# GpSimd makes four of z's sixteen low parts instead of VectorE

## The chip, the core and the metric

The kernel runs on one core of a Trainium2 chip (trn2). Its time is the device time of one execution in microseconds. The engines are called PE (TensorE), DVE (VectorE), ACT (ScalarE), GpSimd or POOL, and SP (the queue that issues most DMAs). They run on their own and meet only at semaphores.

## The reference

The input x is (32, 64, 1024). Two blocks are added to it in turn:

```python
x = x + attn(cond(x, cond_128, ...), w_attn, w_proj, adapter_wte, gating)
x = x + ffn(cond2(x, cond_128, ...), W_base, b_base, W_router, A, B)
```

`cond` mixes the 64 channels of each batch entry with a 64x64 matrix of its own (a softmax over 8 expert matrices, from a small MLP on cond_128) and adds a bias: `out = einsum('boi,bih->boh', agg_w, x) + agg_b`. Its result is called z here: 2048 tokens (32 batches of 64) by 1024. `attn` projects z to q, k and v (1024 to 3 x 1024), rotates q and k, does causal attention over the 64 tokens of each batch entry with 32 heads of 32, adds attention to ten adapter rows, and projects back. `cond2` is a grouped convolution along the 1024, and `ffn` a 1024x1024 layer with a top-2 choice of rank-16 adapters. Everything is float32.

## The kernel before, in words

PE multiplies in the reduced format fp32r. To keep float32's precision, a big operand is split in a high part (a copy rounded to fp32r) and a low part (the float32 value minus the high part), and each product is three matmuls: high by high, high by low, low by high (`split_passes`, line 80). So each piece of z needs a high and a low part in SBUF before it can be projected.

**z in sixteen pairs.** z is made two batch entries at a time: pair i, for i from 0 to 15, is 128 partitions by 1024. Four pairs make a unit u of 512 tokens: unit 0 is pairs 0 to 3, unit 1 is 4 to 7, unit 2 is 8 to 11, unit 3 is 12 to 15. A pair takes four steps on three engines:

- mix i, on PE (lines 269 to 281): 32 small products (64 matmul records) of x with the mixing matrix, into PSUM. It waits for x by DMA and for add i-2 (`wait(pe, z_sum, i - 1)`), since pairs alternate over two sets of PSUM banks. It counts z_mm up.
- add i, on DVE (lines 357 to 369): PSUM plus bias, to f_z_raw in SBUF. One instruction of 1024 for even i (line 363), two of 512 for odd i (line 367). It counts z_sum up.
- high i, on ACT (lines 317 to 319): copy of f_z_raw to fp32r in z. It waits for add i and counts z_hi up.
- low i, on DVE (lines 371 to 373): f_z_raw minus the high part, to z, all three tiles in SBUF. It waits for high i and counts z_lo up.

**The order on PE** is written out by hand. `first_step` (lines 1085 to 1099) does mixes 0 to 5, waits for the lows of unit 0 (`split(0)`), and then projects unit 0 of the first weight group to K, Q and V in eight chunks each; behind every second chunk stands another mix: 6 to 9 in K, 10 to 13 in Q, 14 and 15 in V. Between Q and V lies the small product `project_adapter`. Afterwards `unit_step` (lines 981 to 1001) runs 31 times, for 8 weight groups g by 4 units u: for g = 0 it waits first for the lows of its unit (`mix_tensor.split`, line 283), then come the attention scores of the unit before (lines 893 to 908, which wait for the rotated q and k and for a_avs), the transposes of v (line 964, which wait for ACT's copy vT), the projections K and Q, the transposes of the softmax's results (lines 913 and 920), the projection V, and the products of attention and values (line 935). Each projection is 24 matmuls of 128x512 (line 952). After the attention follow 16 groups of matmuls for the output projection and the ffn (line 1030).

**The order on DVE** is that of its instructions in the code: `mix_on(0, UP)` and the next lines (1345 to 1354) do adds 0 to 4 and lows 0 to 3; `unit_step` with n = 0 does adds 5 to 10 with lows 4 to 9 (line 1619), the rotation of K (`rotate`, lines 1364 to 1382: a product of PSUM and cosine, line 1372; a shuffle out of PSUM, 1374; a product of two SBUF tiles, 1377; a sum of two SBUF tiles, 1380 or 1382), adds 11 to 14 each followed by the low before it (line 1628), the rotation of Q, add 15 (line 1633), the three small instructions a_avs, a_avh, a_avbd (lines 1646 to 1651), and low 14 (line 1655). With n = 1 come the softmax of unit 0 (`attend_softmax`, lines 1384 to 1430: for two halves a masked sum out of PSUM, 1396, a maximum, 1399, a subtraction of two SBUF operands, 1401, and so on to 1430), both rotations and low 15 (line 1635).

**The order on ACT**: highs 0 to 3, a copy of Q's weights, highs 4 to 6, a copy of V's, highs 7 to 10 (lines 1160 to 1167), then in `unit_step` with n = 0 highs 11 to 13, a small copy, high 14, another, high 15 (line 1274), and vT (line 1282), which PE's transposes wait for.

**The order on GpSimd** (lines 856 to 886): a small clear, the low parts w_lo of the three weight blocks (line 379, each after ACT's high part), a clear of aprob once eight adds are done, a clear of vbd once all sixteen mixes are done (line 865; ACT's first copies into vbd wait for it), and then nothing until the ffn, where it adds a bias to 16 tiles (line 879).

**SP** loads x pair by pair into four buffers (a load waits for the mix that frees its buffer), and after the last mix three constants (lines 671 to 673).

Of the kernel before, what the change touches and what calls it, by code (L numbers as in the profile page):

```python
# [27 lines left out]
ALU = mybir.AluOpType  # L28
# [13 lines left out]
UP = UB // 2  # L42
KC = L // P
NP = NB // 2
# [23 lines left out]
Q_, K_, V_ = 0, 1, 2  # L68
MLP_COLS = (NB, P, 1, P, 1, NM, NC)
MIX_COLS = (OB * NC, P // NM)  # L70
DMA_RING = 1024


def wait(eng, sem, value):

    if not isinstance(value, int) or value > 0:
        eng.wait_ge(sem, value)
# [20 lines left out]
def split_columns(t, widths):  # L98

    ends = np.cumsum(widths)  # L100
    return [t[:, int(e - w):int(e)] for w, e in zip(widths, ends)]


def mixing(nc, ctx, d, psum, z, z_f, z_raw, ctx_dram, aggb_dram, first_weights, places):
# [8 lines left out]
    def sem(name):  # L113
        return ctx.enter_context(nc.semaphore(name))
# [15 lines left out]
    sb = Space(nc, "m", small_at).take  # L130
    mix = sb("mix", [P, sum(MIX_COLS)])
    mixw, pick = split_columns(mix, MIX_COLS)
    h0 = sb("h0", [P, NB])
# [35 lines left out]
    z_sum = sem("m_z_sum")  # L169
    z_hi = sem("m_z_hi")  # L170
    z_lo = sem("m_z_lo")
    NCONST = 5
    HALVES = ((0, UP), (UP, NP))

    def slot_bank(i, b):

        return bank[(0, 1, 2, 4)[2 * (i % 2) + b]]

    def z_place(z, i, part):

        return z[:, i // UP, part, :, i % UP * P:(i % UP + 1) * P]
# [42 lines left out]
    class Tensor:  # L224
# [6 lines left out]
        def begin(pe):  # L231
# [9 lines left out]
            pe.wait_ge(mlp_act, 2)  # L241
            pe.wait_ge(consts, 16 * NCONST)
            pe.wait_ge(ones_set, 1)
# [37 lines left out]
            mm.then_inc(z_mm, 1)  # L281

        def split(pe, u):
            pe.wait_ge(z_lo, UP * (u + 1))

    class Scalar:

# [33 lines left out]
    class Vector:  # L321

        def begin(dve):
            dve.memset(busy[:].bitcast(F32), 1.0).then_inc(busy_set, 1)
            dve.memset(ones[:], 1.0).then_inc(ones_set, 1)
            dve.wait_ge(consts, 16 * NCONST)
            dve.wait_ge(ctx_mm, 1)
# [47 lines left out]
    class Pool:  # L375

        def weight_lo(pool, x):
            pool.wait_ge(w_hi[x], 1)
            pool.tensor_tensor(wlo[:, :, x, :], wst[:, :, x, :], whi_f[:, :, x, :], ALU.subtract).then_inc(w_lo[x], 1)

    return (Sync, Pool, Tensor, Scalar, Vector), ctx_out, z_mm, z_sum


def program(nc, d, psum, z, zbase, y_dram, x1_dram, w_forms, ctx_dram, aggb_dram, weights, out):
# [8 lines left out]
    with ExitStack() as ctx:  # L393
        def sem(name):
            return ctx.enter_context(nc.semaphore(name))
# [146 lines left out]
        y_out = sem("a_y_out")  # L542
        NCONST, NCLEAR, NFCONST = 10, 3, 3

# [57 lines left out]
        mix_sync, mix_pool, mix_tensor, mix_scalar, mix_vector = parts  # L602
# [3 lines left out]
        def first(g, u):  # L606
            return isinstance(g, int) and g == 0 and u == 0
# [4 lines left out]
        def refill(g, u):  # L612

            return u == NU - 1 and not last(g)
# [5 lines left out]
        def prep_at(n):  # L620

            g, u = n // NU, n % NU
            return 2 * g + u - 1 if u in (1, 2) else None
# [9 lines left out]
        def plain(f):  # L633

            t, half = {A11: (0, 0), A12: (0, 1), A21: (1, 0), A22: (1, 1)}[f]
            return raw[:, t, KH * half:KH * (half + 1), :]
# [16 lines left out]
        def form_count(order, f, G):  # L653

            return sum(len(order(i)) for i in range(G)) + order(G).index(f) + 1
# [200 lines left out]
        @block.gpsimd  # L856
        def _(pool):
            pool.memset(wte[:, KC * NA:], 0.0).then_inc(cleared, 1)
            mix_pool.weight_lo(pool, K_)
            mix_pool.weight_lo(pool, Q_)  # L860
            mix_pool.weight_lo(pool, V_)
            pool.wait_ge(z_sum, 2 * UP)
            pool.memset(aprob[:].bitcast(F32), 0.0).then_inc(cleared, 1)
            pool.wait_ge(z_mm, NP)
            pool.memset(vbd[:], 0.0).then_inc(cleared, 1)


            def add_bias(G, t):
                if G == NJ and t == 0:
                    pool.wait_ge(row1_set, 2)  # L870
                elif G == NJ:
                    pool.wait_ge(row2_set, 1)
                elif t == 0:
                    pool.wait_ge(x_in[0], 16 * G)
                    pool.wait_ge(row1_set, 2 * G - 1)
                else:
                    pool.wait_ge(x_in[1], 16 * G)
                    pool.wait_ge(v2_set, G)
                pool.tensor_tensor(xn[:, t, :].rearrange("p (m q) -> p q m", q=PH),  # L879
                                   x1[:, t, :].rearrange("p (q m) -> p q m", q=PH),  # L880
                                   bbase[:].rearrange("p (m q) -> p q m", q=PH), ALU.add).then_inc(xn_set, 1)

            pool.wait_ge(fconsts, 16 * NFCONST)
            for G in range(NJ, 2 * NJ):
                for t in range(2):
                    add_bias(G, t)

        @block.tensor
        def _(pe):
# [77 lines left out]
            def project_adapter(g, n):  # L967
                if g == 0:
                    pe.wait_ge(consts, 16 * NCONST)
                    pe.wait_ge(cleared, 1)  # L970
# [372 lines left out]
        def _(dve):  # L1343
            mix_vector.begin(dve)
            def mix_on(i0, i1):

                for i in range(i0, i1):
                    mix_vector.add(dve, i)
                    if i:
                        mix_vector.low(dve, i - 1)  # L1350

            mix_on(0, UP)
# [3 lines left out]
            def split_lo(x, g, n):  # L1356
                dve.wait_ge(w_hi[x], g + 1)
                wait(dve, mm_done[x], n)
                if x != Q_:
                    wait(dve, akv_mm, g)  # L1360
                dve.tensor_tensor(wlo[:, :, x, :], wst[:, :, x, :], whi_f[:, :, x, :], ALU.subtract
                                  ).then_inc(w_lo[x], 1)
# [69 lines left out]
            def prep_sums(k):  # L1432

                dve.wait_ge(prep_in, 32 * (k + 1))
                part = prep_raw

                def take(dst, a, b, done):
                    wait(dve, prep_sum, done)
                    dve.tensor_tensor(part[:, dst, :], part[:, a, :], part[:, b, :], ALU.subtract).then_inc(prep_sum, 1)

                take(T3, B22, T1, 0)
                take(T1, T1, B11, 0)
                take(T2, B22, T1, 4 * k + 2)
                take(T4, B21, T2, 4 * k + 3)
# [29 lines left out]
            def low(G, f):  # L1474
                dve.wait_ge(act_hi_set, form_count(form_order, f, G))
                src = act_sum[f][:] if f in (S1, S2, S4, S3) else plain(f)
                dve.tensor_tensor(act_lo[f][:], src, act_hi[f][:].bitcast(F32), ALU.subtract).then_inc(act_set, 1)  # L1477
# [138 lines left out]
            def unit_step(g, u):  # L1616
                n = NU * g + u
                if n == 0:
                    mix_on(UP + 1, NP - 5)
                if n == 1:  # L1620
                    dve.wait_ge(cleared, 2)
                if not first(g, u):
                    attend_softmax(n - 1)
                if n == 0:
                    dve.wait_ge(consts, 16 * NCONST)
                rotate(K_, bK, kr, n, ((scores, 2 * n),), n)
                if n == 0:
                    mix_on(NP - 5, NP - 1)
                if prep_at(n) is not None:
                    prep_sums(prep_at(n))  # L1630
                rotate(Q_, bQ, qr, n, ((scores, 2 * n),), n)
                if n == 0:
                    mix_vector.add(dve, NP - 1)
                if n == 1:
                    mix_vector.low(dve, NP - 1)
                    dve.memset(x8[0][0:P // 2, :, 0:1], 0.0).then_inc(edges, 1)
                    dve.memset(x8[0][P // 2:P, :, L // PH:L // PH + 1], 0.0).then_inc(edges, 1)
                if refill(g, u):
                    split_lo(K_, g + 1, n + 1)
                    split_lo(Q_, g + 1, n + 1)  # L1640
                    split_lo(V_, g + 1, n + 1)
                if u == 0:

                    dve.wait_ge(akbd_set, g + 1)
                    wait(dve, avbd_set, g)
                    dve.tensor_tensor(avs[:], bAD[:, AVS:AVS + P], amask[:], ALU.mult).then_inc(avs_set, 1)
                    dve.wait_ge(avs_set, g + 1)
                    dve.tensor_scalar(avh[:], avs[:], alow[:, 0:1], None, ALU.mult).then_inc(avh_set, 1)
                    dve.wait_ge(avh_set, g + 1)
                    wait(dve, y_mm, n)  # L1650
                    dve.tensor_tensor(avbd[:], avs[:], avh[:].bitcast(F32), ALU.subtract).then_inc(avbd_set, 1)
                if prep_at(n) is not None:
                    prep_low(prep_at(n))
                if n == 0:
                    mix_vector.low(dve, NP - 2)
                if n == NG * NU - 1:
                    first_forms()

# [189 lines left out]
```

## Time and profile before

| what | us |
|---|---|
| median of three runs | 1139.5 |
| lowest and highest of the three | 1138.58, 1141.15 |
| the profiled execution, its own time | 1137.45 |
| its span, first to last instruction | 1135.7 |

| engine | busy us | share of the span | instructions |
|---|---|---|---|
| PE | 1122.7 | 99% | 9400 |
| DVE | 919.0 | 81% | 1737 |
| ACT | 359.4 | 32% | 665 |
| GpSimd | 60.1 | 5% | 26 |

Times in the trace are microseconds from the start of the span. The busy time of PE is modelled from pipelined matmuls. The name of an engine behind an idle time is what released the instruction, as the semaphore events show it.

### The profile page before, as it was taken

To read this page: it belongs to the slowest core of one execution; us is meant where nothing else is said; L and a number is where in the kernel's file an instruction comes from. 1 tells how busy PE (TensorE), PEld (TensorE's weight loads), DVE (VectorE), ACT (ScalarE), POOL (GpSimd) and SP (SyncE) were. 2 spreads that over 40 slices of the span, in tenths; PEclk is the share of its full clock that TensorE was granted. 3 is DMA by queue.
4 is the path that set the end of the run, shared out by engine and by line. 5 is a ranking of instruction groups with operands and counts; after the bars stand their busy time and mean duration, and the time that the engine had idled before them with its cause. 6 is when DMAs were issued, how large, how long until landed. Compare 5 with 4: busy or idle time off the path is not lost.

```text
span 1135.7 us, 23010 instructions
## 1 busy us (share of the span) xinstructions
PE 1122.7 (99%) x9400; PEld 937.6 (83%) x9400; DVE 919.0 (81%) x1737; ACT 359.4 (32%) x665; POOL 60.1 (5%) x26
## 2 busy tenths in 40 slices
PE   7999999999999999999999999999999999999998
PEld 5778888888888888888888888878888888888887
DVE  5999889789789798798798899888767767887765
ACT  5443332342432433433334334323222221222210
POOL 1100000000000000000000000110000022221112
PEclk9999999999999999999999999999999999999999
DMA  6525124024034033033123277884559933233312
GB/s 221 187 79 158 54 72 161 30 91 161 10 105 147 16 116 131 23 110 131 38 94 131 66 271 263 323 246 156 185 130 354 336 95 102 96 116 116 99 38 93
DMA packets 99706, 151.91 MB, mean 134 GB/s; under 512 B 7442, under 2 KB 84114, under 8 KB 96914
## 3 DMA queue, kind: packets, MB, share of 16 engines
q1 hardware_dynamic: 98594, 135.76, 36.9%
q10 hardware_dynamic: 1008, 14.68, 3.1%
q8 instruction: 75, 1.23, 0.5%
q14 instruction: 29, 0.24, 0.1%
HBM read 95.88 MB, written 54.54 MB: 132 GB/s over the span
## 4 chain that ended last, share of the span: by engine, by line
PE 89%; DVE 6%; issue 2%; DMA 2%; ACT 1%; SPq 0%; DVEq 0%; ACTq 0%
PE psum L952 43%; PE psum L1030 23%; PE psum L1048 5%; PE psum L935 3%; PE psum L920 2%; PE psum L904 2%; PE psum L1082 2%; PE psum L1064 2%; DMA y_scratch<-a_ysb 2%; PE psum L964 2%; DVE z L373 1%; PE psum L913 1%; PE psum L1066 1%; DVE f_z_raw L367 1%; PE psum L976 1%
## 5 line engine op out<-in xcount | busy, mean ns | idle before, releaser
L952 PE MATMUL psum<-z,w_hi 128*128 128x512 f32 x1536 | 481.8, 395 | 1.1 <-DVE z L373 1.1
L952 PEld LDWEIGHTS psum<-z,w_hi 128*128 128x128 f32 x1536 | 282.4, 188 | 58.6 <-DVE z L373 1.2
L952 PE MATMUL psum<-z,w_lo 128*128 128x512 f32 x768 | 300.5, 391 | 0.0
L1030 PE MATMUL psum<-f_wform,f_act_hi 128*128 128x512 f32 (+1 forms) x912 | 279.9, 389 | 1.3 <-DVE f_u L1496 1.2
L1030 PEld LDWEIGHTS psum<-f_wform,f_act_hi 128*128 128x128 f32 x912 | 167.9, 188 | 35.9 <-issue 2.7
L1030 PE MATMUL psum<-f_wform,f_act_lo 128*128 128x512 f32 (+1 forms) x456 | 176.1, 386 | 0.0
L952 PEld LDWEIGHTS psum<-z,w_lo 128*128 128x128 f32 x768 | 144.1, 188 | 30.6
L879 POOL TENSOR_TENSOR f_xn<-f_x,_bbase 128x1024 f32<-128x1024 f32 x16 | 51.1, 3194 | 1009.3 <-DVE f_x L1522 679.6
L1030 PEld LDWEIGHTS psum<-f_wform,f_act_lo 128*128 128x128 f32 x456 | 85.6, 188 | 17.6
L1222 ACT ACTIVATE f_act_hi<-f_act_sum 128x512 fp32r<-128x512 f32 x64 | 40.3, 632 | 119.2 <-DVE f_act_sum L1471 47.9
L1222 ACT ACTIVATE f_act_hi<-f_raw 128x512 fp32r<-128x512 f32 x56 | 33.7, 626 | 103.1 <-DVE f_raw L1554 64.8
L1396 DVE TENSOR_TENSOR a_prob<-psum,a_mask 128x512 f32<-128x512 f32 x64 | 44.0, 687 | 26.7 <-PE psum L904 26.7
L1477 DVE TENSOR_TENSOR f_act_lo<-f_act_sum,f_act_hi 128x512 fp32r<-128x512 f32 x64 | 49.0, 768 | 16.7 <-ACT f_act_hi L1222 16.7
L1477 DVE TENSOR_TENSOR f_act_lo<-f_raw,f_act_hi 128x512 fp32r<-128x512 f32 x56 | 37.2, 688 | 28.3 <-ACT f_act_hi L1222 28.2
L1187 ACT ACTIVATE a_aT<-psum 128x512 fp32r<-128x512 f32 x32 | 19.2, 600 | 122.0 <-PE psum L913 121.8
L1295 ACT ACTIVATE a_vbd<-psum 64x256 f32<-64x256 f32 x128 | 48.5, 379 | 26.2 <-PE psum L964 25.1
L1180 ACT ACTIVATE a_prob<-a_prob 128x512 f32<-128x512 f32 x64 | 40.5, 633 | 51.4 <-DVE a_prob L1401 50.9
L1374 DVE STREAM_SHUFFLE a_rot<-psum 128x512 f32<-128x512 f32 x64 | 47.1, 737 | 0.0
L1413 DVE TENSOR_TENSOR a_prob<-a_prob,a_stat 128x512 f32<-128x512 f32 x64 | 44.3, 692 | 2.2
L1401 DVE TENSOR_TENSOR a_prob<-a_prob,a_stat 128x512 f32<-128x512 f32 x64 | 44.3, 692 | 2.2
L1377 DVE TENSOR_TENSOR a_rot<-a_rot,a_sin 128x512 f32<-128x512 f32 x64 | 44.3, 692 | 2.2
L1399 DVE TENSOR_REDUCE a_stat<-a_prob 128x8 f32<-128x512 f32 x64 | 44.0, 687 | 2.2
(172 smaller groups left out, 1466.0 us busy)
## 6 DMA issues: line engine op xcount, KB each, us to landing
w_forms<-f_prep_lo SPq DMA_DIRECT2D x16, 896.0 KB, 5.1
f_wform<-w_forms SPq DMA_DIRECT2D x7, 2048.0 KB, 13.6
f_wform<-w_forms ACTq DMA_DIRECT2D x7, 2048.0 KB, 18.8
w_st<-in_wqkvT SPq DMA_DIRECT2D x7, 1536.0 KB, 6.6
w_forms<-f_prep_hi SPq DMA_DIRECT2D x16, 640.0 KB, 6.4
m_x<-in_x SPq DMA_DIRECT2D x16, 512.0 KB, 5.4
y_scratch<-a_ysb SPq DMA_DIRECT2D x32, 256.0 KB, 2.7
f_raw<-y_scratch SPq DMA_DIRECT2D x8, 1024.0 KB, 5.9
```

Source lines behind the costliest of these rows:

```text
L879: pool.tensor_tensor(xn[:, t, :].rearrange("p (m q) -> p q m", q=PH), x1[:, t, :].rearrange("p (q m) -> p q m", q=PH), bbase[:].rearrange( ...
L952: mm = pe.matmul(dst, w[:, c, x, :], zs, start=(c == 0 and i == 0), stop=(c == KC - 1 and i == 2))
L1030: mm = pe.matmul((prod_bank[i], bank[0])[part][:, cols], a[:, c, :], wform[i][:, w, c, cols], start=(i < 4 and c == 0 and n == 0), stop=(c ...
L1048: mm = pe.matmul(conv_banks(p)[:, o:o + P], x8[p % 2][:, CONV * b + g, j:j + P], toep[:, g, j, :], start=(j == 0), stop=(j == 1))
L1222: act.activation(act_hi[f][:], src, ACT.Copy).then_inc(act_hi_set, 1)
L1295: cp = act.activation(vbd[NC * h:NC * (h + 1), :, b, :, HD * h:HD * (h + 1)], bV[NC * b:NC * (b + 1), :].rearrange("p (s a h e) -> p s a h ...
L1374: dve.stream_shuffle(rot[:], src[:], HALF_SWAP).then_inc(turned[x], 1)
L1377: dve.tensor_tensor(r, r, tab[1], ALU.mult).then_inc(rot_step, 1)
L1396: dve.tensor_tensor(prob[t][:].rearrange("p (s h) k -> p h s k", h=2), score_slots[:, 2 * t:2 * t + 2, :, 0:NC], maskb, ALU.add).then_inc( ...
L1401: dve.tensor_tensor(prob[t][:], prob[t][:], spread(t, 0), ALU.subtract).then_inc(shifted, 1)
L1413: dve.tensor_tensor(prob[t][:], prob[t][:], spread(t, 2), ALU.mult).then_inc(probs, 1)
L1477: dve.tensor_tensor(act_lo[f][:], src, act_hi[f][:].bitcast(F32), ALU.subtract).then_inc(act_set, 1)
```

## The change

Pairs 10, 12, 14 and 15 get their low part from GpSimd, by the same subtraction on the same tiles, and DVE leaves them out. GpSimd's lows 10 and 12 stand between its clear of aprob and its wait for the last mix; lows 14 and 15 stand behind its clear of vbd. They count a semaphore of their own, z_lo_pool, and PE waits for both counts before a unit of z is projected.

```diff
--- before.py
+++ after.py
@@ -68,6 +68,8 @@
 Q_, K_, V_ = 0, 1, 2
 MLP_COLS = (NB, P, 1, P, 1, NM, NC)
 MIX_COLS = (OB * NC, P // NM)
+POOL_LOWS = (10, 12, 14, 15)
+DVE_LOWS = (0, 1, 2, 3, 4, 5, 6, 7, 8, 9, 11, 13)
 DMA_RING = 1024
 
 
@@ -169,12 +171,17 @@
     z_sum = sem("m_z_sum")
     z_hi = sem("m_z_hi")
     z_lo = sem("m_z_lo")
+    z_lo_pool = sem("m_z_lo_pool")
     NCONST = 5
     HALVES = ((0, UP), (UP, NP))
 
     def slot_bank(i, b):
 
         return bank[(0, 1, 2, 4)[2 * (i % 2) + b]]
+
+    def lows(engine, count):
+
+        return sum(i in engine for i in range(count))
 
     def z_place(z, i, part):
 
@@ -281,7 +288,8 @@
             mm.then_inc(z_mm, 1)
 
         def split(pe, u):
-            pe.wait_ge(z_lo, UP * (u + 1))
+            pe.wait_ge(z_lo, lows(DVE_LOWS, UP * (u + 1)))
+            wait(pe, z_lo_pool, lows(POOL_LOWS, UP * (u + 1)))
 
     class Scalar:
 
@@ -377,6 +385,10 @@
         def weight_lo(pool, x):
             pool.wait_ge(w_hi[x], 1)
             pool.tensor_tensor(wlo[:, :, x, :], wst[:, :, x, :], whi_f[:, :, x, :], ALU.subtract).then_inc(w_lo[x], 1)
+
+        def low(pool, i):
+            pool.wait_ge(z_hi, i + 1)
+            pool.tensor_tensor(z_place(z, i, 1), raw_place(i), z_place(z_f, i, 0), ALU.subtract).then_inc(z_lo_pool, 1)
 
     return (Sync, Pool, Tensor, Scalar, Vector), ctx_out, z_mm, z_sum
 
@@ -861,8 +873,12 @@
             mix_pool.weight_lo(pool, V_)
             pool.wait_ge(z_sum, 2 * UP)
             pool.memset(aprob[:].bitcast(F32), 0.0).then_inc(cleared, 1)
+            mix_pool.low(pool, 10)
+            mix_pool.low(pool, 12)
             pool.wait_ge(z_mm, NP)
             pool.memset(vbd[:], 0.0).then_inc(cleared, 1)
+            mix_pool.low(pool, 14)
+            mix_pool.low(pool, 15)
 
 
             def add_bias(G, t):
@@ -1346,7 +1362,7 @@
 
                 for i in range(i0, i1):
                     mix_vector.add(dve, i)
-                    if i:
+                    if i - 1 in DVE_LOWS:
                         mix_vector.low(dve, i - 1)
 
             mix_on(0, UP)
@@ -1632,7 +1648,6 @@
                 if n == 0:
                     mix_vector.add(dve, NP - 1)
                 if n == 1:
-                    mix_vector.low(dve, NP - 1)
                     dve.memset(x8[0][0:P // 2, :, 0:1], 0.0).then_inc(edges, 1)
                     dve.memset(x8[0][P // 2:P, :, L // PH:L // PH + 1], 0.0).then_inc(edges, 1)
                 if refill(g, u):
@@ -1651,8 +1666,6 @@
                     dve.tensor_tensor(avbd[:], avs[:], avh[:].bitcast(F32), ALU.subtract).then_inc(avbd_set, 1)
                 if prep_at(n) is not None:
                     prep_low(prep_at(n))
-                if n == 0:
-                    mix_vector.low(dve, NP - 2)
                 if n == NG * NU - 1:
                     first_forms()
```

## Rows read from the trace of the kernel before

**Rows 1.** The page, busy time and share of the span by engine.

```profile
PE 1122.7 (99%) x9400; PEld 937.6 (83%) x9400; DVE 919.0 (81%) x1737; ACT 359.4 (32%) x665; POOL 60.1 (5%) x26
```

**Rows 2.** Busy time by stretch: stretch, its length, engines (instructions), granted clock, DMA.

```profile
20.00:25.00 5.00, 2.58 (x133) 2.23 (x132) 4.95 (x6) 2.25 (x4) 0.00 (x0) 1.00 0.86 286
...
80.00:100.00 20.00, 20.00 (x185) 16.80 (x184) 19.28 (x41) 7.62 (x15) 0.00 (x0) 1.00 0.42 133
```

**Rows 3.** Timeline of PE: start, length, line and work, count, idle before.

```profile
1.45 2.50 PE L229 MATMUL psum<-m_busy 128*128 128x512 f32 x5 [1.45 <-DVE m_busy L324]
...
48.65 1.16 PE L279 MATMUL psum<-m_aggT,m_x 64*64 64x64 f32 x64
...
52.33 1.16 PE L279 MATMUL psum<-m_aggT,m_x 64*64 64x64 f32 x64
...
55.01 1.16 PE L279 MATMUL psum<-m_aggT,m_x 64*64 64x64 f32 x64
...
59.19 0.39 PE L952 MATMUL psum<-z,w_lo 128*128 128x512 f32 x1
60.35 0.93 PE L904 MATMUL psum<-a_kbd,a_qr 32*64 32x74 f32 x64 [0.77 <-DVE a_avs L1646]
61.64 0.66 PE L964 MATMUL psum<-_ident,a_vT 128*128 128x128 f32 x4 [0.35 <-ACT a_vT L1282]
...
73.07 0.60 PE L913 MATMUL psum<-_ident,a_aprob 128*128 128x128 f32 x4
```

**Rows 4.** Timeline of DVE, from K's rotation to the end of the softmax.

```profile
45.48 0.69 DVE L1377 TENSOR_TENSOR a_rot<-a_rot,a_sin 128x512 f32<-128x512 f32 x1
...
46.82 1.28 DVE L367 TENSOR_TENSOR f_z_raw<-psum,m_aggb 128x512 f32<-128x512 f32 x2
48.02 1.21 DVE L373 TENSOR_TENSOR z<-f_z_raw,z 128x1024 fp32r<-128x1024 f32 x1
49.15 1.22 DVE L363 TENSOR_TENSOR f_z_raw<-psum,m_aggb 128x1024 f32<-128x1024 f32 x1
...
53.75 1.22 DVE L363 TENSOR_TENSOR f_z_raw<-psum,m_aggb 128x1024 f32<-128x1024 f32 x1
...
57.39 0.69 DVE L1377 TENSOR_TENSOR a_rot<-a_rot,a_sin 128x512 f32<-128x512 f32 x1
...
59.92 0.28 DVE L1646 TENSOR_TENSOR a_avs<-psum,a_amask 128x128 f32<-128x128 f32 x1
...
61.90 0.68 DVE L1396 TENSOR_TENSOR a_prob<-psum,a_mask 128x512 f32<-128x512 f32 x1
...
71.50 0.24 DVE L1430 CAST a_aprob<-a_aprob 128x160 fp32r<-128x160 f32 x1
```

**Rows 5.** Timeline of ACT, highs 10 and 15.

```profile
43.09 1.06 ACT L319 ACTIVATE z<-f_z_raw 128x1024 fp32r<-128x1024 f32 x1 [1.25 <-DVE f_z_raw L363]
...
60.04 1.06 ACT L319 ACTIVATE z<-f_z_raw 128x1024 fp32r<-128x1024 f32 x1 [3.05 <-DVE f_z_raw L367]
```

**Rows 6.** Timeline of GpSimd: the last w_lo and the two clears.

```profile
33.84 2.36 POOL L379 TENSOR_TENSOR w_lo<-w_st,w_hi 128x1024 fp32r<-128x1024 f32 x1 [4.48 <-ACT w_hi L315]
36.13 0.53 POOL L863 MEMSET a_aprob<- 128x512 f32 x1
56.26 0.95 POOL L865 MEMSET a_vbd<- 128x1024 f32 x1 [19.60 <-PE psum L279]
```

**Rows 7.** Timelines of DVE and GpSimd where their instructions overlap.

```profile
26.86 2.50 POOL L379 TENSOR_TENSOR w_lo<-w_st,w_hi 128x1024 fp32r<-128x1024 f32 x1 [12.16 <-ACT w_hi L315]
...
28.14 1.28 DVE L367 TENSOR_TENSOR f_z_raw<-psum,m_aggb 128x512 f32<-128x512 f32 x2
...
33.97 3.31 DVE L373 TENSOR_TENSOR z<-f_z_raw,z 128x1024 fp32r<-128x1024 f32 x1
...
740.10 3.44 POOL L879 TENSOR_TENSOR f_xn<-f_x,_bbase 128x1024 f32<-128x1024 f32 x1 [3.14 <-DVE f_x L1522]
...
741.30 2.78 DVE L1477 TENSOR_TENSOR f_act_lo<-f_act_sum,f_act_hi 128x512 fp32r<-128x512 f32 x1 [0.76 <-ACT f_act_hi L1222]
```

## The prediction

> **What bounds the kernel now.** I read the page first: TensorE is busy for 1122.7 of 1135.7 us, so the kernel is a string of matmuls with 13 us of holes in it [rows 1]. The stretches say where the holes lie: from 20 to 25 us PE worked 2.58 of 5 us, from 80 to 100 us all of 20.00 [rows 2]. After unit 1 begins there is nothing to win, and anything that shifts PE before then shifts the end by as much. The change touches work between 44 and 80 us, so the question is what PE waits for there. The timeline of PE has two waits in it: 0.77 us before the first attention scores (line 904), which DVE's a_avs (line 1646) ends, and 0.35 us before the transposes of line 964, which ACT's copy vT ends [rows 3]. DVE is continuously busy there, in the order add 11, low 10, ..., add 14, low 13, Q's rotation (lines 1372 to 1382), add 15, a_avs, low 14, softmax [rows 4]. At best the change takes 1.1 us out of PE.
>
> **What it moves.** Lows 10, 12, 14 and 15 (line 373: two SBUF inputs, 1.21 us; the next instruction starts 1.13 us after it, at 49.15 against 48.02 [rows 4]) leave DVE: 4 x 1.13 = 4.5 us less work. GpSimd does them instead, each 128x1024 fp32r from f32 with two SBUF inputs. That is the shape of w_lo, 2.36 us [rows 6], and it works on nothing else there. So 4 x 2.36 = 9.4 us, on an engine that was idle for 19.6 us before its vbd clear.
>
> **The price of it.** GpSimd and DVE don't run such instructions together. While GpSimd made w_lo from 33.84 to 36.20, DVE's low, begun at 33.97, took 3.31 instead of 1.21 us; at 740.10 GpSimd's sum ran 3.44 us, to 743.54, and DVE's 128x512 subtraction of two SBUF tiles took 2.78 us and ended at 744.08, 0.54 us behind it [rows 7]. An instruction with one input in PSUM is not held: the adds at 28.14 took 1.28 us inside a GpSimd instruction of 26.86 to 29.36 [rows 7], the same as at 46.82 [rows 4]. So each GpSimd low costs DVE nothing if adds or waits lie beside it, and up to 2.36 us if two-SBUF work does. The Trainium skill, page SBUF — State Buffer, section "SBUF: two separate sides", speaks against this change: the port pair of the two is an exclusive lock, whoever starts first keeps it for the whole instruction, and a DVE instruction with two SBUF inputs is subject to it. The trace agrees, with the 3.31 us.
>
> **Low 10.** ACT's high 10 ends at 43.09 + 1.06 = 44.15 [rows 5]. GpSimd follows a semaphore by 0.09 us (mix 15 ends at 55.01 + 1.16 = 56.17, the clear starts at 56.26 [rows 3, 6]): 44.24 to 46.60. DVE is then in K's rotation; the first two steps read PSUM, the third (line 1377, at 45.48, ends 46.17 [rows 4]) reads two SBUF tiles and is held to 46.60 + 0.54 = 47.14: +0.97. Add 11 moves by it, from 46.82 to 47.79, and ends at 49.07. PE follows a DVE end by 0.15 us (a_avs ends 60.20, scores 60.35 [rows 3, 4]), and mix 13 needs add 11: 49.22 instead of 48.65, PE +0.57. GpSimd's clear of vbd needs mix 15 alone, so it moves with PE.
>
> **Low 12.** DVE skips low 10 and does add 12 (48.99 to 50.21) and low 11 (to 51.34). High 12 on ACT ends at 50.21 + 0.03 + 1.06 = 51.30, GpSimd runs 51.39 to 53.75, beside add 13 (PSUM) and an idle DVE: nothing. The freed time is not used either, since add 14 must wait for mix 14, which ends at 52.33 + 1.16 + 0.57 = 54.06 [rows 3]. So add 14 starts at 54.14 instead of 53.75 [rows 4]: +0.39, in spite of two lows less on DVE.
>
> **Low 14.** Behind add 14 come low 13 and Q's rotation, all +0.39, so line 1377 would start at 57.39 + 0.39 = 57.78 [rows 4]. GpSimd: mix 15 ends at 56.17 + 0.57 = 56.74, the clear starts 0.09 later at 56.83, lasts 0.95 us, and its successor starts 0.07 us ahead of its end (36.13 behind 33.84 + 2.36 [rows 6]): 57.71 to 60.07. Line 1377 falls onto it and ends at 60.07 + 0.54 = 60.61 instead of 58.08: +2.53. Should DVE be a hair first, line 1382, 0.04 us behind, is held instead, and the sum is within 0.1 us of the same: both engines are set by mixes 14 and 15, so this is no matter of luck. Add 15 and a_avs follow at once, the scores start at 60.35 + 2.53 = 62.88, and PE, which is there at 59.58 + 0.57 = 60.15 [rows 3], waits 2.7 us in place of 0.77. ACT's high 15 stands ahead of vT in its queue and waits for add 15 [rows 5], so vT and the transposes at 61.64 also move by 2.5.
>
> **Low 15, and what is late next.** High 15 then ends at 60.04 + 1.06 + 2.53 = 63.63, and GpSimd runs 63.72 to 66.08. DVE's softmax begins at 61.90 + 2.53 - 1.13 (low 14) = 63.30 [rows 4]; its third instruction (line 1401, two SBUF inputs, 1.4 us later) is held by about 1.2 us. Its last, at 71.50 + 0.24 = 71.74, becomes 71.74 + 1.40 + 1.2 = 74.3, and PE wants it at 73.07 + 2.53 = 75.6 [rows 3, 4]: 1.3 us left, cost nothing. The highs and lows themselves are wanted no earlier than unit 2, behind the last of rows 3. No DMA moves but SP's constants behind mix 15, 0.6 us later, with nothing waiting.
>
> **Sum.** 0.39 + 2.14 = +2.5 us on PE, of which the saturated stretches give nothing back. The profiled execution took 1137.45 us (span 1135.7), 2.05 below the median of 1139.5; the same sum on the median gives 1142.0. The GpSimd duration is the term to doubt. From row w_lo it is 2.36 us. The Trainium skill, page GPSIMD Engine Reference, section "Performance versus the Vector engine", gives 4497 ns for a two-input f32 sum of 2048 elements; half of that, an estimate, is 2.25 us, and the sum would be about 2.4 us. Bounds for the collision from rows: nothing, and a full 2.36 + 0.1 us; for low 10's, 0 to 1.0 us on DVE. I take the computed overlap for both, as 33.97 and 741.30 behave so to 0.1 us.
>
> **Rivals.**
> (a) Low 14 misses the rotation, so the kernel is not slower. Its place is lines 1377 and 1382, its condition that GpSimd's low begins after 59.2 instead of 57.7. For it: GpSimd starts late if its wait or its clear is slower than the rows; against: the clear's and w_lo's rows leave 1.5 us to make up. Then only +0.39 stays: 1139.9. Chance 0.20.
> (b) The two engines don't exclude each other on these tiles. DVE then gains only until mix 14 (which ends at 53.49): Q's rotation starts 0.16 us earlier: 1139.3. Against it stand all of rows 7. Chance 0.04.
> (c) PE's clock falls in the 2.7 us wait, the longest since the start; with 2.58 of 5 us busy it held 1.00, i.e. 2.4 GHz [rows 2]. A 128x512 matmul took 2.50 / 5 = 0.5 us at the beginning [rows 3], against (73.07 - 61.64) / 48, at most 0.24, in unit 1. Eight matmuls at that rate: +2.1, so 1144.1. Chance 0.06. The Trainium skill, page TensorE: Matmul & The Clock Gate, Part 1, has the clock fall to 1.2 GHz after idling; no row here shows a fall.
> (d) Low 15 holds softmax for its full 2.36 and more, and the transposes wait 1.1 us: 1143.1. Chance 0.04.
>
> **Numbers.** Forecast 1142.0, chance 0.66, own range 1141.3 to 1142.8. About 0.2%, 2.3 us, is what a measurement can tell from no change (the three runs lie 2.6 us apart), and +2.5 is just above it: of the 0.66 I give 0.42 to slower, 0.24 to same. With (c) and (d) slower is 0.52; with (a) and (b), less 0.03 for scatter, same is 0.45; faster 0.03, since no case reaches -2.3. The range takes in (b) below and stops between (d) and (c): 1139.3 to 1143.6.
>
> **What would show it.** On DVE, one instruction at line 1377 or 1382 of 2 to 3 us in Q's rotation, and one of about 1.7 us in K's, each over a GpSimd low; PE's wait at line 904 at about 2.7 us; lows of 2.36 us at about 44, 51, 58 and 64 us; no other wait longer on PE. I am wrong if that wait stays under 1 us, if the lows last over 3 us, or if PE's matmuls after 63 us are slower than 0.24 us.

## The result, and the profile after

The changed kernel takes 1142.91 us in the median of 22 runs, the kernel before 1138.63 us in 22 runs on the same chips. The ratio is 1.0031, with a 95% interval of 1.0025 to 1.0038: 3.5 us slower, between 2.8 and 4.3. (The two medians alone lie 4.3 us apart.) One run of the changed kernel, of 3394.87 us, is left out of the ratio. The forecast was +2.5 us and 1142.0 us.

The profiled execution of the changed kernel took 1142.84 us (span 1141.0), against 1137.45 us before. That is 5.4 us, more than the ratio. The whole of it lies ahead of 79 us, in two pieces, which one mark separates: the first step of K's rotation on DVE, the last instruction ahead of anything that the change can touch. It starts at 44.10 us before and at 45.66 after; those 1.6 us belong to the start, in work that both kernels share (the 16 matmuls at 10.95 us took 3.50 us in place of 2.91, and later PE waited 2.0 us for loads of x in place of 1.0). In the eight experiments below, the same step starts anywhere from 44.81 to 49.85 us. From that step to the transposes of line 913 (929 after), where PE is saturated again, the kernel before needs 73.07 - 44.10 = 28.97 us and the changed one 78.60 - 45.66 = 32.94 us. **The change costs 3.97 us in this trace**, and all that follows has to explain that number.

The page, busy time by engine, of the changed kernel, for rows 1:

```profile
PE 1125.8 (99%) x9400; PEld 940.4 (82%) x9400; DVE 916.8 (80%) x1733; ACT 359.2 (31%) x665; POOL 69.2 (6%) x30
```

Four instructions and 2.2 us have left DVE, four and 9.1 us have come to GpSimd. DVE lost 4 x 1.22 us of lows, so more than half of that came back as longer instructions. Where they are, the timelines of GpSimd and DVE tell. GpSimd first, all that it starts between 38 and 80 us (line 391 is the low, before line 373):

```profile
38.85 0.54 POOL L875 MEMSET a_aprob<- 128x512 f32 x1
45.78 2.38 POOL L391 TENSOR_TENSOR z<-f_z_raw,z 128x1024 fp32r<-128x1024 f32 x1 [6.38 <-ACT z L327]
52.92 2.40 POOL L391 TENSOR_TENSOR z<-f_z_raw,z 128x1024 fp32r<-128x1024 f32 x1 [4.77 <-ACT z L327]
58.39 0.95 POOL L879 MEMSET a_vbd<- 128x1024 f32 x1 [3.06 <-PE psum L286]
59.30 2.40 POOL L391 TENSOR_TENSOR z<-f_z_raw,z 128x1024 fp32r<-128x1024 f32 x1
65.34 2.36 POOL L391 TENSOR_TENSOR z<-f_z_raw,z 128x1024 fp32r<-128x1024 f32 x1 [3.64 <-ACT z L327]
```

And DVE, for rows 4 (line 1393 was 1377, line 1417 was 1401):

```profile
47.05 1.66 DVE L1393 TENSOR_TENSOR a_rot<-a_rot,a_sin 128x512 f32<-128x512 f32 x1
...
52.90 1.28 DVE L375 TENSOR_TENSOR f_z_raw<-psum,m_aggb 128x512 f32<-128x512 f32 x2
55.69 1.23 DVE L371 TENSOR_TENSOR f_z_raw<-psum,m_aggb 128x1024 f32<-128x1024 f32 x1 [1.51 <-PE psum L286]
...
58.57 0.74 DVE L1390 STREAM_SHUFFLE a_rot<-psum 128x512 f32<-128x512 f32 x1
59.34 2.90 DVE L1393 TENSOR_TENSOR a_rot<-a_rot,a_sin 128x512 f32<-128x512 f32 x1
62.28 0.69 DVE L1398 TENSOR_TENSOR a_qr<-a_qr,a_rot 128x512 f32<-128x512 f32 x1
...
66.97 1.28 DVE L1417 TENSOR_TENSOR a_prob<-a_prob,a_stat 128x512 f32<-128x512 f32 x1
```

The reader should lay these two over each other. The same product of line 1393 takes 1.66 us while GpSimd makes low 10, and 2.90 us while it makes low 14, instead of 0.69 both times; the second ends at 62.24, 0.54 us behind GpSimd's 61.70. The adds at 52.90, with PSUM as an input, take 1.28 us inside GpSimd's low 12, as ever. And in front of the add at 55.69, DVE idles 1.51 us for mix 14: the time that lows 10 and 12 left free. PE, for rows 3:

```profile
50.77 1.16 PE L286 MATMUL psum<-m_aggT,m_x 64*64 64x64 f32 x64 [0.51 <-DVE f_z_raw L375]
...
64.51 0.93 PE L920 MATMUL psum<-a_kbd,a_qr 32*64 32x74 f32 x64 [2.81 <-DVE a_avs L1661]
65.80 1.11 PE L980 MATMUL psum<-_ident,a_vT 128*128 128x128 f32 x4 [0.35 <-ACT a_vT L1298]
66.56 1.20 PE L968 MATMUL psum<-z,w_hi 128*128 128x512 f32 x2
67.56 0.63 PE L968 MATMUL psum<-z,w_lo 128*128 128x512 f32 x1
67.99 0.98 PE L968 MATMUL psum<-z,w_hi 128*128 128x512 f32 x2
68.81 0.39 PE L968 MATMUL psum<-z,w_lo 128*128 128x512 f32 x1
...
78.60 0.60 PE L929 MATMUL psum<-_ident,a_aprob 128*128 128x128 f32 x4
```

The wait for the scores grew from 0.77 to 2.81 us. Behind it stands what the forecast had as its rival (c) and left out of its sum: the four transposes take 1.11 instead of 0.66 us, and the first matmuls of the projection 1.20 and 0.63 us, where those at 68.81 are back at 0.39. From the transposes of line 964's kind to those of line 913's there is the same work and no wait: 73.07 - 61.64 = 11.43 us before, 78.60 - 65.80 = 12.80 us after, so 1.37 us. The view by stretches shows why (columns as in rows 2; the granted clock is the third number from the right):

```profile
61.00:65.00 4.00, 1.19 (x47) 0.75 (x49) 3.90 (x7) 0.80 (x1) 0.70 (x1) 1.00 0.92 350
65.00:69.00 4.00, 3.65 (x47) 3.05 (x40) 3.39 (x6) 2.74 (x7) 2.36 (x1) 0.57 0.02 4
69.00:73.00 4.00, 4.00 (x19) 3.26 (x19) 3.86 (x8) 1.08 (x3) 0.00 (x0) 1.00 0.00 0
```

PE worked 1.19 of 4 us, and in the next 4 us the clock granted was 0.57 of full speed, near its lower level of 1.2 GHz (0.50), before it went back to 2.4 GHz. The 3.97 us are then: 0.57 at mix 13, 2.04 more of wait at the scores, 1.37 of clock, 3.98 together.

### The profile page after: what moved, and what is told of

The parts are those of the page before. It is cut to its first block, busy times and chain, and to the rows that moved or that the text cites. A ratio compares the mean times of both kernels' runs of the same rounds, so it can differ in the third digit from the quotient of the medians.

```text
span 1141.0 us, 23010 instructions
## 1 busy us (share of the span) xinstructions
PE 1125.8 (99%) x9400; PEld 940.4 (82%) x9400; DVE 916.8 (80%) x1733; ACT 359.2 (31%) x665; POOL 69.2 (6%) x30
## 4 chain that ended last, share of the span: by engine, by line
PE 90%; DVE 4%; DMA 2%; issue 2%; SPq 1%; ACT 0%; DVEq 0%; ACTq 0%
PE psum L968 44%; PE psum L1046 23%; PE psum L1064 5%; PE psum L951 3%; PE psum L936 2%; PE psum L920 2%; PE psum L1098 2%; PE psum L1080 2%; DMA y_scratch<-a_ysb 2%; PE psum L980 2%; PE psum L929 1%; PE psum L286 1%; PE psum L1082 1%; PE psum L992 1%; PE psum L236 1%
## 5 line engine op out<-in xcount | busy, mean ns | idle before, releaser
L1393 DVE TENSOR_TENSOR a_rot<-a_rot,a_sin 128x512 f32<-128x512 f32 x64 | 47.5, 742 | 2.2
```

Of the source, the lines that this page charges most:

```text
L1393: dve.tensor_tensor(r, r, tab[1], ALU.mult).then_inc(rot_step, 1)
```

## The experiments

The main theory: GpSimd's lows and DVE's products of two SBUF tiles exclude each other, low 14 falls on Q's rotation, PE waits, and the long wait also lowers PE's clock. The rivals: low 10 carries the loss; the clock costs nothing and the rest is chance; or any move to GpSimd loses. Each ratio below is against the kernel before on the same chips. The stage is the time from the first step of K's rotation on DVE to the softmax transposes on PE in the one profiled execution of each kernel, so it has no interval; before it is 28.97 us.

| kernel | ratio, 95% interval | expected | PE's wait at the scores | stage, against before |
|---|---|---|---|---|
| the change | 1.0031 (1.0025 to 1.0038) | | 2.81 | +3.97 |
| lows 10 and 12 alone | 0.9999 (0.9990 to 1.0008) | 1.0003 | 0.58 | +0.37 |
| lows 14 and 15 alone | 1.0030 (1.0018 to 1.0041) | 1.0029 | 2.82 | +3.63 |
| low 14 behind Q's rotation | 1.0006 (0.9995 to 1.0017) | 1.0003 | 0.61 | +0.90 |
| the change, wait filled | 1.0023 (1.0014 to 1.0032) | 1.0022 | none | +2.67 |
| before, DVE held up by clears | 1.0035 (1.0021 to 1.0048) | 1.0031 | 3.23 | +4.14 |
| the same, wait filled | 1.0020 (1.0011 to 1.0029) | 1.0018 | 0.69 | +2.63 |
| change, reordered | 0.9988 (0.9978 to 0.9998) | 0.9991 | none | -0.37 |
| before, low 13 later | 0.9991 (0.9982 to 1.0000) | 0.9992 | none | -1.13 |

### Which of the four lows costs it

```diff
-POOL_LOWS = (10, 12, 14, 15)
+POOL_LOWS = (10, 12)
...
-            mix_pool.low(pool, 14)
-            mix_pool.low(pool, 15)
...
+                    mix_vector.low(dve, NP - 1)
...
+                if n == 0:
+                    mix_vector.low(dve, NP - 2)
```

> GpSimd makes lows 10 and 12 alone; DVE makes 14 and 15 where it did before. Theory (GpSimd's low 14 collides with Q's rotation, and PE's long wait that follows also lowers its clock): low 14 is gone, so line 1393 in Q's rotation takes 0.69 us, line 1393 in K's still about 1.7 us, PE waits about 0.6 us at the scores, and the time is 0.4 us over before (ratio 1.0003). Rival 1 (low 10's collision in K's rotation carries the loss): the ratio stays near 1.003. Rival 2 (the profile after began later for reasons of its own, and the change costs only 2.5 us all told): cannot be told apart here.

The time is that of the kernel before: 0.9999. DVE's timeline has the collision with low 10 all the same (line 1391 is the product of line 1377 before):

```profile
46.95 1.67 DVE L1391 TENSOR_TENSOR a_rot<-a_rot,a_sin 128x512 f32<-128x512 f32 x1
...
59.26 0.69 DVE L1391 TENSOR_TENSOR a_rot<-a_rot,a_sin 128x512 f32<-128x512 f32 x1
```

PE lost 0.6 us at mix 13 and got 0.2 of it back at the scores, where it waited 0.58 in place of 0.77 us; the rest is the +0.37 us of its stage. So rival 1 falls: the held product costs DVE 1 us and the kernel at most the 0.4 us of this stage, where the change costs 4.0. The other half:

```diff
-POOL_LOWS = (10, 12, 14, 15)
+POOL_LOWS = (14, 15)
...
-            mix_pool.low(pool, 10)
-            mix_pool.low(pool, 12)
```

> GpSimd makes lows 14 and 15 alone; DVE keeps 10 and 12. Theory: mix 15 ends as before, low 14 starts about 0.3 us ahead of line 1393 in Q's rotation, which ends 2.0 us late; PE's wait at the scores is 2.7 us and its clock falls in the matmuls behind it, for another 1.3 us: 3.3 us over before (ratio 1.0029). Rival 1 (low 10 carries the loss): ratio under 1.001. Rival 2 (no cost of the clock): 2.0 us, ratio 1.0018.

1.0030, the whole loss of the change; low 15 stands in it too, but the trace shows nothing on PE that waits for it. PE's timeline around its wait is that of the change:

```profile
64.93 0.93 PE L918 MATMUL psum<-a_kbd,a_qr 32*64 32x74 f32 x64 [2.82 <-DVE a_avs L1659]
66.22 1.11 PE L978 MATMUL psum<-_ident,a_vT 128*128 128x128 f32 x4 [0.35 <-ACT a_vT L1296]
```

So is the stretch behind it, with a granted clock of 0.66:

```profile
65.00:70.00 5.00, 4.65 (x76) 3.93 (x77) 4.35 (x7) 3.31 (x7) 2.37 (x1) 0.66 0.03 9
```

### The same work on GpSimd, a little later

```diff
+            pool.wait_ge(rotated[Q_], 1)
             mix_pool.low(pool, 14)
             mix_pool.low(pool, 15)
```

> All four lows stay on GpSimd, but low 14 first waits until Q's rotation is done. GpSimd does the same work, 1.5 us later. Theory: nothing in Q's rotation is held, PE waits about 0.6 us at the scores, the clock stays, and low 14 and 15 lie beside the small adapter steps and the softmax, which have 1.3 us to spare: 0.4 us over before (ratio 1.0003). Rival 3 (the loss is GpSimd's traffic or its lateness, not this collision): ratio stays near 1.003. Rival 4 (the collision moves to the softmax and delays the transposes by more than its slack): 1.0010 or more, with a wait of PE at line 929.

1.0006, with an interval that holds both 1.0003 and 1, and not the 1.0031 of the change. All four lows are on GpSimd, so it is not the move that costs but where low 14 falls. Rival 4 has a small share: lows 14 and 15 now run back to back, and hold what stands behind a_avs on DVE, as DVE's timeline shows:

```profile
66.09 0.28 DVE L1662 TENSOR_TENSOR a_avs<-psum,a_amask 128x128 f32<-128x128 f32 x1
66.41 1.10 DVE L1664 TENSOR_SCALAR a_avh<-a_avs,a_alow 128x128 fp32r<-128x128 f32 x1
67.55 2.37 DVE L1667 TENSOR_TENSOR a_avbd<-a_avs,a_avh 128x128 fp32r<-128x128 f32 x1
```

GpSimd's timeline of the same kernel has the two lows as one entry:

```profile
65.05 4.71 POOL L391 TENSOR_TENSOR z<-f_z_raw,z 128x1024 fp32r<-128x1024 f32 x2 [1.51 <-DVE a_qr L1399]
```

a_avh waited for the first of the two to end, slipped in between, and a_avbd waited for the second: two waits for two GpSimd instructions, 0.28 and 0.29 us of work. The softmax was late by so much that the transposes on PE waited 0.31 us for it.

### The clock, twice

The wait itself was left as it is, and filled with work:

```diff
+                if n == 1:
+                    pe.wait_ge(z_sum, NP - 1)
+                    for _ in range(12):
+                        pe.matmul(bank[0], whi[:, 0, K_, :], z[:, 0, 0, 0, :], start=True, stop=True)
                 if att:
                     attend_scores(n - 1, groups)
```

> The kernel of the change, with twelve extra matmuls of 128x512 on PE in the place where it waits for the scores of unit 0 (about 2.8 us of work into a PSUM bank that the scores overwrite); the results are unchanged. Theory (clock): PE isn't idle there, its granted clock stays at 1.00 from 65 to 70 us, the matmuls behind the wait keep 0.23 us, and 1.3 us come back: 2.6 us over before (ratio 1.0022). Rival 2 (no cost of the clock): nothing comes back, ratio as the change, 1.0031, or more if the filling is longer than the wait.

1.0023. DVE is as late as in the change (its product in Q's rotation takes 2.90 us again), and PE does 2.9 us of useless matmuls more; yet its ratio is 0.8 thousandths below that of the change. The intervals of the two overlap, so the times alone would not settle it. The timeline of PE does (line 1006 is the filling):

```profile
61.35 2.88 PE L1006 MATMUL psum<-z,w_hi 128*128 128x512 f32 x12
64.32 0.93 PE L920 MATMUL psum<-a_kbd,a_qr 32*64 32x74 f32 x64
65.61 0.66 PE L980 MATMUL psum<-_ident,a_vT 128*128 128x128 f32 x4 [0.35 <-ACT a_vT L1302]
...
77.06 0.60 PE L929 MATMUL psum<-_ident,a_aprob 128*128 128x128 f32 x4
```

The stretch that had 0.57 in the changed kernel now reads:

```profile
65.00:69.00 4.00, 3.65 (x44) 2.97 (x28) 3.57 (x5) 2.70 (x7) 2.39 (x1) 1.00 0.02 4
```

The clock stays at 1.00, and from transposes to transposes it is 77.06 - 65.61 = 11.45 us, the 11.43 of the kernel before. So 1.37 us of the 3.97 are the clock. The same pair was then made out of the kernel before, with none of the moved work on GpSimd; the filled one has the twelve matmuls from above as well:

```diff
+                if n == 0:
+                    for k in range(4):
+                        dve.memset(qr[:], 0.0).then_inc(again, 1)
+                        dve.wait_ge(again, k + 1)
                 rotate(Q_, bQ, qr, n, ((scores, 2 * n),), n)
```

> The kernel before, with four clears of 128x512 on DVE ahead of Q's rotation in unit 0 (some 0.5 us each, of a tile that the rotation writes anyway), and nothing on GpSimd. It makes PE's wait of the change without the change. Theory (wait and clock, whatever makes DVE late): Q's rotation is 2.0 to 2.2 us late, PE waits 2.8 to 3.0 us at the scores, its clock falls right behind, 1.4 us more: 3.4 to 3.6 us over before, ratio 1.0031. Rival 2 (no cost of the clock): 2.1 us, 1.0018. Rival 3 (the loss needs GpSimd): less than 1 us.

> The run above, with the twelve extra matmuls on PE in the place of the wait. Theory: DVE as late as above, PE not idle, granted clock 1.00 throughout, from the transposes of line 964's kind to those of the softmax 11.4 us as before: 2.1 us over before, ratio 1.0018. Rival 2: as the run above.

1.0035 and 1.0020. A wait made by four clears on DVE costs what the change costs. Rival 3, that the loss needs GpSimd, falls with it. The filled kernel's ratio is 1.5 thousandths lower; the intervals overlap here too, so the traces have to decide. In PE's timeline of the first, the wait is 3.23 us, and this time even the scores are slow:

```profile
64.21 1.38 PE L905 MATMUL psum<-a_kbd,a_qr 32*64 32x74 f32 x64 [3.23 <-DVE a_avs L1651]
65.52 1.11 PE L965 MATMUL psum<-_ident,a_vT 128*128 128x128 f32 x4
```

The filled one waited 0.69 us at the scores, behind the filling, and held 1.00 from 60 to 75 us. The clears were mis-sized: with the waits between them they take 0.66 us each and make Q's rotation 2.6 us late, not 2.1. So the filled one should cost 2.6 us and does in its stage (+2.63; its ratio of 1.0020 is 2.3 us).

Of the 1.5 us between the two stages, the clock has 1.0: from the transposes of v to those of the softmax it is 77.92 - 65.52 = 12.40 us in the unfilled kernel and 11.43 in the filled one. The other 0.5 us is an accident of the unfilled trace: mix 13 on PE came in two pieces, with idle time between (see the last section), so mix 14 and with it add 14 on DVE came late, 10.16 us behind K's first step instead of 9.65:

```profile
54.97 1.22 DVE L363 TENSOR_TENSOR f_z_raw<-psum,m_aggb 128x1024 f32<-128x1024 f32 x1 [0.42 <-PE psum L279]
```

Whether the timed runs have it as well isn't known.

### Without the wait

```diff
+            pool.wait_ge(rotated[K_], 1)
             mix_pool.low(pool, 10)
...
+            pool.wait_ge(rotated[Q_], 1)
             mix_pool.low(pool, 14)
...
-                    mix_on(NP - 5, NP - 1)
+                    mix_on(NP - 5, NP - 2)
...
                 if n == 0:
+                    mix_on(NP - 2, NP - 1)
                     mix_vector.add(dve, NP - 1)
```

> The change with three moves: GpSimd's low 10 waits for K's rotation, its low 14 for Q's, and DVE does Q's rotation ahead of add 14, in the time in which it waits for mix 14. Theory: nothing in a rotation is held, the rotated q and a_avs are ready before PE's unit 0 ends, PE has neither the 0.77 nor the 0.35 us of wait: 1.0 to 1.1 us less than before, ratio 0.9991, which may not be told from 1. If low 12, which starts when low 11 ends, still meets line 1377's kind in Q's rotation, up to 0.3 us are lost on DVE and none on PE. Rival (a move of work off DVE cannot pay, since the port is held for 2.4 us per low): ratio over 1.001.

0.9988, interval 0.9978 to 0.9998: faster than both kernels, by 1.4 us against the one before. The interval ends close to 1, so the gain is small and only just shown. Q's rotation now stands where DVE would idle for mix 14, and PE meets neither wait. DVE's timeline:

```profile
55.48 0.69 DVE L1395 TENSOR_TENSOR a_rot<-a_rot,a_sin 128x512 f32<-128x512 f32 x1
...
60.48 0.28 DVE L1664 TENSOR_TENSOR a_avs<-psum,a_amask 128x128 f32<-128x128 f32 x1
60.80 1.91 DVE L1666 TENSOR_SCALAR a_avh<-a_avs,a_alow 128x128 fp32r<-128x128 f32 x1
62.74 2.37 DVE L1669 TENSOR_TENSOR a_avbd<-a_avs,a_avh 128x128 fp32r<-128x128 f32 x1
```

And PE's, from the scores to the softmax transposes, with no idle time ahead of any:

```profile
62.54 0.94 PE L922 MATMUL psum<-a_kbd,a_qr 32*64 32x74 f32 x64
63.42 0.66 PE L982 MATMUL psum<-_ident,a_vT 128*128 128x128 f32 x4
...
74.90 0.66 PE L931 MATMUL psum<-_ident,a_aprob 128*128 128x128 f32 x4
```

GpSimd still holds a_avh and a_avbd here, for 3.7 us together, and PE's matmuls don't wait for that. There is no slack left, though: the softmax's last step on DVE (line 1448) ends at 74.85 us, and the weight load of the transposes waited 0.35 us for it, hidden behind a matmul that was still running. And the last kernel moves no work to GpSimd at all:

```diff
-                    mix_on(NP - 5, NP - 1)
+                    mix_on(NP - 5, NP - 2)
+                    mix_vector.add(dve, NP - 2)
...
                 if n == 0:
+                    mix_vector.low(dve, NP - 3)
                     mix_vector.low(dve, NP - 2)
```

> The kernel before, all lows on DVE, with low 13 moved from ahead of Q's rotation to behind a_avbd. No work moves to GpSimd. Theory (the wait of PE was one of order): Q's rotation, add 15 and a_avs come 1.13 us earlier, PE's two waits of 0.77 and 0.35 us go, the softmax starts as before and has 0.2 us to spare: 0.8 to 1.1 us less than before, ratio 0.9992. Rival: the softmax is late for the transposes of line 913 and the gain is given back there, ratio 1.000.

0.9991, interval 0.9982 to 1.0000, at its edge. The stage is 27.84 us, 1.13 less than before, as worked out. Sharing the work with GpSimd and moving one instruction on DVE are not told apart by their times; what both do is to get q and a_avs ready before PE asks for them.

## Why the prediction was right, and by which step it fell short

Slower was forecast and slower it is; 1142.91 us lies 0.9 above the forecast and inside the range of 1139.3 to 1143.6, and 0.1 above the narrower one of 1141.3 to 1142.8 that the prediction gave its main case. That the time came so close is in part luck: the forecast stood on a median of three runs, 1139.5, and 22 runs give 1138.63. The difference is the better test, and there +2.5 was forecast and +3.5 measured, with an interval (2.8 to 4.3) that leaves 2.5 out. The case that came true is the main one together with rival (c), not the main one alone.

- **The exclusion of the two engines**: right, where lows 10, 14 and 15 meet a DVE instruction with two SBUF inputs (1.66, 2.90 and 1.28 us in place of 0.69), and right for the adds beside low 12 (1.28 us, as ever). GpSimd's lows took 2.36 to 2.40 us against 2.36 from the row of w_lo. The estimate of 2.25 us, half of what the Trainium skill, page GPSIMD Engine Reference, section "Performance versus the Vector engine", gives for twice the elements, was 0.11 to 0.15 us too short; the row was the better source.
- **Low 10**: right. The held product took 1.66 us, as worked out (0.69 + 0.97), and mix 13 came 3.26 us behind mix 12 instead of 2.69: +0.57, the number forecast.
- **Low 12 and the idle DVE**: right. Add 14 starts 10.03 us behind the first step of K's rotation instead of 9.65, +0.38 against a forecast of +0.39, and DVE idles in front of it.
- **Low 14**: right, with 2.90 us for the held product against 2.83, and 2.81 us for PE's wait against 2.7. That low 14 and the rotation meet by the order of the program and not by luck is borne out: the product took 2.90, 2.85 and 2.90 us in the three traces that have low 14 in this place, whose starts differ by 1 us (the changed kernel, lows 14 and 15 alone, the wait filled).
- **Low 15**: hidden, as forecast, though it held the softmax's subtraction by 0.6 and not 1.2 us, since DVE first waited 0.5 us for the scores. The last step of the softmax was done 2.7 us before the transposes; 1.4 of that is PE's slower clock, and without it the 1.3 forecast is left.
- **The step that failed** is the one that kept the clock at 1.00 through the wait and gave (c) a chance of 0.06. It rested on rows 2, where PE worked 2.58 of 5 us at full clock. Here the wait was 2.81 us, and the granted clock fell to 0.57 of full speed in the next 4 us. It cost 1.37 us, where (c) had put 2.1 from eight matmuls at the pace of the first five. The prediction's own sign for this, matmuls slower than 0.24 us behind 63 us, came up: two that take 0.71 us before took 1.20, and the next 0.63 in place of 0.40. The Trainium skill, page TensorE: Matmul & The Clock Gate, Part 1, has the clock fall after idling. The traces agree: it fell behind the waits at the scores of 2.81, 2.82 and 3.23 us, at a cost of 1.37, 1.48 and 0.97 us from transposes to transposes, and held behind those of 0.8 us and less. In between, the length of a wait doesn't decide it. Three rows of PE from the starts of the changed kernel, of the clears, and of the clears filled show this:

```profile
20.95 3.66 PE L286 MATMUL psum<-m_aggT,m_x 64*64 64x64 f32 x126 [1.99 <-issue]
...
19.84 2.42 PE L279 MATMUL psum<-m_aggT,m_x 64*64 64x64 f32 x81 [1.44 <-issue]
...
27.39 1.49 PE L279 MATMUL psum<-m_aggT,m_x 64*64 64x64 f32 x83 [2.22 <-issue]
```

Behind 1.99 us the granted clock was 0.50 (22 to 24 us), behind 1.44 us it was 0.50 (20 to 22 us), and behind 2.22 us it was 1.00 (27 to 29 us). What decides between the two levels stays open.
- **The sum** was 2.5; the parts it named come to 2.6 in the trace (0.57 + 2.04), and the run that keeps them and takes the clock's part away has 1.0023, which is 2.6 us. With 1.37 for the clock the trace gives 4.0, the ratio 3.5 with an interval of 2.8 to 4.3.

## What to carry to other kernels

Before work is moved from DVE to GpSimd, lay GpSimd's instructions over DVE's timeline: here each was free beside DVE's adds, which read PSUM (1.28 us), and beside waits, and held work with two SBUF inputs for up to 2.2 us (2.90 in place of 0.69 us), and only a collision on the way to something that PE waits for is paid. Look also at what DVE would do with the time it gains; here it waited for the next mix, and two changes of order came out 1.4 and 1.0 us below the time before (the second at the edge of its interval), where the same four lows off DVE, in the order of the change, came out 3.5 us above. When a wait of PE grows, look at the granted clock behind it: waits of 2.8 to 3.2 us cost another 1.0 to 1.5 us here, and the two that were filled with matmuls cost nothing behind them.

## What was not expected of the hardware

- Where GpSimd's lows 14 and 15 follow each other at once (low 14 behind Q's rotation, and the reordered kernel), DVE got one instruction in between them, and waited again: in the reordered kernel a_avh took 1.91 us and a_avbd 2.37 us, for 0.28 and 0.29 us of work. a_avh has one SBUF tile and a column of scalars as inputs, and was held too. A reduction with one SBUF tile as input was not: the softmax's maximum at 66.25 us took 0.69 us in the changed kernel, as ever, with GpSimd's low 15 running from 65.34 to 67.70.
- PE sometimes loses up to 0.9 us inside mix 13 with nothing shown that it waits for. In PE's timeline of the reordered kernel the mix comes in two pieces:

```profile
50.83 1.03 PE L286 MATMUL psum<-m_aggT,m_x 64*64 64x64 f32 x52
52.40 0.45 PE L286 MATMUL psum<-m_aggT,m_x 64*64 64x64 f32 x12 [0.54 <-issue]
```

It ends 2.0 us after its start, not 1.16. This is in four of the ten traces (lows 14 and 15 alone, the clears, the reordered kernel, low 13 later), of kernels with the change and without it. It delays what follows only where PE has no time to spare: by 0.5 us in the stage of the clears and by 0.8 us in that of the reordered kernel, whose -0.37 would be about -1.2 without it (an estimate from its 1.94 us between the starts of mix 13 and of the next matmuls, in place of 1.09). In the other two, mix 13 had started 0.4 us earlier and the next matmuls came on time. The cause of it stays open.
